# A decoder layer in one kernel: sums of the 64-key softmaxes on GpSimd and logarithms subtracted, the landmark-query softmax transposed, and x1 in place

## The reference

```python
q_l = q.reshape(b, h, m, l, dh).mean(axis=3)          # m = 64 landmarks
k_l = k.reshape(b, h, m, l, dh).mean(axis=3)
attn1 = softmax(q @ k_l.T)                            # 512 tokens x 64 landmark keys
attn2 = softmax(q_l @ k_l.T)                          # 64 x 64
attn3 = softmax(q_l @ k.T)                            # 64 landmark queries x 512 keys
for _ in range(6):                                    # V starts as attn2
    KV = attn2 @ V
    V = 0.25 * V @ (13 * I - KV @ (15 * I - KV @ (7 * I - KV)))
x = x + (attn1 @ (V @ (attn3 @ v))) @ Wout + bout
# cross attention, keys and values from ctx_1024 (64 keys a batch)
scores = where(mask == 0, -1e9, Q @ K.T / sqrt(16))
x = x + (softmax(scores) @ V) @ Wo.T + bo
# feed-forward: sel = argmax(gelu(last @ Wp1 + bp1) @ Wp2 + bp2)
h = gelu(x_norm @ W1[sel] + b1[sel])
x = x + x_norm + 0.3 * ((h @ W2[sel] + b2[sel]) @ Wo_ffn + bo_ffn)
```

## Time and profile before

| | |
|---|---|
| median of three runs | 1453.8 us (1453.03 to 1455.01) |
| the profiled execution | 1456.06 us |
| its span in the trace | 1454.3 us |
| mean granted TensorE clock | 0.992 |
| TensorE busy in the span | 1418.4 us |
| VectorE, ScalarE, GpSimd busy | 1016.4, 752.0, 571.5 us |

### The profile page before, as it was taken

The page is one execution under the profiler, slowest core; times in us unless marked ns, Lnnn a source line. Parts: engine busy times, 40 slices in busy tenths (PEclk is TensorE's granted clock), DMA queues, the critical chain, the costliest instruction groups (busy, mean ns, idle before and its releaser), DMA issues.

```text
span 1454.3 us, 51361 instructions
## 1 busy us (share of the span) xinstructions
PE 1418.4 (98%) x22484; PEld 943.5 (65%) x22484; DVE 1016.4 (70%) x2098; ACT 752.0 (52%) x1460; POOL 571.5 (39%) x784
## 2 busy tenths in 40 slices
PE   8999999999999999999999999999999999999897
PEld 5756666666757667676666767666676666666455
DVE  2567767767677786767778686777867677588651
ACT  2525563655556465555645555564555636544342
POOL 1525361533526144352524435152453613514423
PEclk9999999999999999999999999999999999999899
DMA  8102000101002010100201010010101001100111
GB/s 301 33 3 76 30 31 2 56 12 42 26 4 64 3 42 26 42 25 2 66 2 42 26 42 25 3 61 7 42 26 42 26 2 43 32 3 3 36 48 61
DMA packets 40527, 53.03 MB, mean 36 GB/s; under 512 B 9698, under 2 KB 30450, under 8 KB 40306
## 3 DMA queue, kind: packets, MB, share of 16 engines
q1 hardware_dynamic: 40306, 49.76, 10.6%
HBM read 37.16 MB, written 12.59 MB: 34 GB/s over the span
## 4 chain that ended last, share of the span: by engine, by line
PE 92%; DVE 3%; DMA 1%; ACT 1%; issue 1%; SPq 1%; POOL 1%; DVEq 0%; POOLq 0%; ACTq 0%
PE bank L1207 43%; PE bank L1439 8%; PE bank L1225 7%; PE bank L1235 6%; PE bank L1426 5%; PE bank L1326 3%; PE bank L1394 2%; PE bank L1215 2%; PE bank L1306 2%; PE bank L1335 2%; PE bank L1285 2%; PE bank L1407 2%; PE bank L1385 1%; PE bank L1320 1%; PE bank L1273 1%; PE bank L1428 1%
## 5 line engine op out<-in xcount | busy, mean ns | idle before, releaser
L675 POOL TENSOR_TENSOR b<-ut,eye 128x256 f32<-128x256 f32 x192 | 136.5, 729 | 343.9 <-DVE ut L1047 281.6
L848 ACT ACTIVATE az<-bank 128x320 f32<-128x320 f32 x192 | 67.4, 401 | 159.5 <-PE bank L1225 157.2
L1207 PE MATMUL bank<-xnT_c,w1e 128*128 128x512 f32 x256 | 125.6, 617 | 1.5 <-DMA b1e<-in_b 0.7
L1207 PE MATMUL bank<-xnT_a,wqkv 128*128 128x512 f32 x256 | 125.0, 612 | 0.1
L1103 DVE RECIPROCAL oT_x<-bank 128x256 f32<-128x256 f32 x64 | 107.9, 1725 | 22.9 <-PE bank L1439 22.9
L1207 PE MATMUL bank<-w2e,hT 128*128 128x256 f32 x512 | 119.7, 388 | 0.9 <-ACT hT L908 0.9
L1103 DVE RECIPROCAL oT<-bank 128x256 f32<-128x256 f32 x64 | 111.9, 1751 | 3.5 <-PE bank L1439 2.9
L796 ACT ACTIVATE p<-bank,nm 128x512 f32<-128x512 f32 x128 | 87.3, 691 | 47.0 <-DVE nm L992 46.9
L574 POOL TENSOR_SCALAR var_eps_c<-mv_c 128x2 f32<-128x2 f32 x32 | 7.2, 225 | 255.0 <-DVE mv_c L928 254.9
L1207 PEld LDWEIGHTS bank<-w2e,hT 128*128 128x128 f32 x512 | 95.8, 192 | 16.1 <-issue 1.7
L1077 DVE TENSOR_REDUCE m<-bank 128x8 f32<-128x512 f32 x128 | 79.9, 682 | 27.5 <-PE bank L1394 26.0
(11 more groups left out here) (212 smaller groups left out, 3198.1 us busy)
## 6 DMA issues: line engine op xcount, KB each, us to landing
x_in<-in_x SPq DMA_DIRECT2D x16, 512.0 KB, 4.0
w1e<-in_W SPq DMA_DIRECT2D x16, 512.0 KB, 3.2
w2e<-w2o SPq DMA_DIRECT2D x16, 512.0 KB, 3.8
out<-base SPq DMA_DIRECT2D x32, 256.0 KB, 3.1
row_e<-w2o_row SPq DMA_DIRECT2D x16, 128.0 KB, 4.7
hT<-in_W2T SPq DMA_DIRECT2D x2, 512.0 KB, 5.8
...
```

The lines of the kernel that those rows point to most:

```text
L675: return g.tensor_tensor(b7[:, q, :], ut[:, q, :], eye[28 if it else 7][:].unsqueeze(1) .broadcast_to([P, 4, LM]), ALU.subtract).then_inc( ...
L1207: last = mm(dst, lhsT, rhs, start=(k == 0), stop=(k == len(pairs) - 1))
```

## The change

**The two softmaxes over 64 keys (suffix 1 and x).** The sum is now taken before the transposed maximum. For each of the 8 tiles of a softmax, VectorE's new step `sb` subtracts the maximum from the scores on the way from PSUM to an SBUF tile `ee` (two tiles in turn), ScalarE's `en` exponentiates in place, and GpSimd's `sm` adds 64 values down to 8 in three additions. VectorE's `es` reduces these, ScalarE's `ln` takes the logarithm, and `mp` adds it to the maximum before it splits it in three. What t and e give is then normalised. The steps den, rec and the multiplication of o are gone; ScalarE copies o out of PSUM. The banks of s1 and sx are emptied by `sb`.

**The landmark queries' softmax.** e3 no longer reads the scores s3 and p3T is gone. The maxima m3 (not negated) are split (`mp3`), transposed (`mT3` on TensorE, copied by VectorE) and subtracted in a product, and `t3` computes the scores transposed, as sx does: one starter per tile with `minus3`, then 16 products. e3 exponentiates straight into `p3T`. vt has a column of ones beside each head's 16, which yields the sum, and zT takes the two heads of a pair one after the other.

**x1 in place.** A second transfer loads x into x1 (`S.x1`, after wx of the batch before), `xr` and `x1b` add their biases in place, and the buffers `xr` and `x1_box` are gone. x1b waits for lnB's readers of x1.

**Once, in the first turns.** `cst` makes `minus3`, sets the ones in vt and zeroes `m3_parts`, and v waits for it; a batch whose mask allows no key gets no mask at all (`any_key`).

**The tables.** TURN and LAST are new throughout, and a batch is spread over six turns. One line of each:

```diff
-    S.fc P.k.0-1 D.mx1.1.3-2 S.f.4-3 A.f.3-1 G.b7.1.0-2 P.iT.1-2 P.iZ.1-2 A.mTx-3 P.kx.1-2 D.mx1.1.2-2
+    S.fc D.wb.5.1-6 S.w2.3-5 D.wb.5.0-6 D.sb1.0.3-5 D.vx-6 G.sm1.0.2-5 P.s1.1-5 P.jZ.5-6 A.nmC.0-7
...
```

The core of the rest:

```diff
+                if kind in ("sm1", "smx"):
...
+                    if c := unmet(pool, "A", i, ("en" + x, k, j)):
+                        pool.wait_ge(act_done, c)
+                    if c := unmet(pool, "D", i - 1, ("es" + x,)):
+                        pool.wait_ge(dve_done, c)
+                    e = ee[x][:, j % 2]
+                    for w in (32, 16):
+                        g.tensor_tensor(e[:, :, :, 0:w], e[:, :, :, 0:w], e[:, :, :, w:2 * w], ALU.add)
+                        g.drain()
+                    return g.tensor_tensor(e8[x][:, :, j, 2 * k:2 * k + 2, :], e[:, :, :, 0:8], e[:, :, :, 8:16],
+                                           ALU.add).then_inc(pool_done, 1)
...
-                    return add_row(xr[:], x_in[:], bout_row).then_inc(pool_done, 1)
+                    return add_row(x1[:], x1[:], bout_row).then_inc(pool_done, 1)
...
-                    return s.activation(p3[:, j], tile(i, ("s3", k), j)[:], ACT.Exp, bias=nm3[:, c:c + 1],
-                                        accum_out=sum3[:, c:c + 1]).then_inc(act_done, 1)
...
+                    return s.activation(p3T[:, j].rearrange("p t c -> p (t c)"), tile(i, ("t3", k), j)[:],
+                                        ACT.Exp).then_inc(act_done, 1)
...
+                if kind in ("en1", "enx"):
...
+                    e = ee[x][:, j % 2].rearrange("p t h c -> p (t h c)")
+                    return s.activation(e, e, ACT.Exp).then_inc(act_done, 1)
+                if kind in ("ln1", "lnx"):
...
+                    return s.activation(esum_ln[x][:].rearrange("p t j c -> p (t j c)"),
+                                        esum[x][:].rearrange("p t j c -> p (t j c)"), ACT.Ln).then_inc(act_done, 1)
+                if kind in ("o1", "ox"):
...
+                    return s.activation(oT[x][:, n, :], tile(i, step)[:], ACT.Copy).then_inc(act_done, 1)
...
+                if kind in ("sb1", "sbx"):
...
+                    return v.tensor_tensor(ee[x][:, j % 2], tile(i, ("s" + x, k), j)[:].rearrange(
+                        "p (t h c) -> p t h c", t=T, h=2), m[x][:, :, j, 2 * k:2 * k + 2].unsqueeze(3)
+                        .broadcast_to([P, T, 2, LM]), ALU.subtract).then_inc(dve_done, 1)
+                if kind in ("es1", "esx"):
...
+                    return v.tensor_reduce(esum[x][:].rearrange("p t j c -> p (t j c)"),
+                                           e8[x][:].rearrange("p t j c e -> p (t j c) e"), AX.X, ALU.add).then_inc(dve_done, 1)
...
+                    v.tensor_tensor(m[x][:], m[x][:], esum_ln[x][:], ALU.add)
...
-                    return v.reciprocal(oT[x][:, k, cols], tile(i, ("den" + x, k))[:, cols]).then_inc(dve_done, 1)
...
-                    return v.tensor_tensor(oT[x][:, n, :], tile(i, step)[:], oT[x][:, n, :], ALU.mult).then_inc(dve_done, 1)
...
-                    dst, res = (x1, xr) if kind == "w1" else (x2, x1_box)
+                    dst, res = (x1, x1) if kind == "w1" else (x2, x1)
...
-                        last = nc.tensor.transpose(o[:, t * P:(t + 1) * P], p3[:, n % 4, t * P:(t + 1) * P], ident[:])
+                    for j in range(4):
+                        mm(tile(i, step, j)[:], minus3[rows(j), :], m3T[rows(j), n, :].unsqueeze(1)
+                           .broadcast_to([32, T, P]), start=True, stop=False)
+                    for t in range(T):
+                        for j in range(4):
+                            last = mm(tile(i, step, j)[:, t * P:(t + 1) * P], kT[rows(j), n, t * P:(t + 1) * P],
+                                      flat(qbd[rows(j), n]), start=False, stop=(t == T - 1))
...
-                    for t in range(T):
-                        for j in range(4):
-                            c = (4 * n + j) * 2 * DH
-                            last = mm(o[rows(j), 0:P], vt[:, t, c:c + 2 * DH], p3T[:, j, t, :],
-                                      start=(t == 0), stop=(t == T - 1))
+                    for h in range(2):
+                        q = slice(LM * h, LM * h + LM)
+                        for t in range(T):
+                            for j in range(4):
+                                last = mm(o[rows(j), q], vt[:, t, 2 * (4 * n + j) + h, :], p3T[:, j, t, q],
+                                          start=(t == 0), stop=(t == T - 1))
```

More of the change, by code:

```diff
@@ L172 @@
+    P.wx.1@15 D.wx.1@15 P.wx.0@15 D.lnC.1@15 G.rsC.1@15 D.wx.0@15 A.nmC.1@15 D.lnC.0@15 P.xnTc.1@15
+    A.xnTc.1@15 P.gate@15 A.gate@15 G.rsC.0@15 A.nmC.0@15 P.logit@15 D.logit@15 G.base@15 P.xnTc.0@15
+    A.xnTc.0@15 S.ew1@15 S.ew2@15 G.row@15 P.h.0@15 P.h.1@15 P.h.2@15 A.h.0@15 A.h.1@15 A.h.2@15
+    P.h.3@15 A.h.3@15 P.y3.1@15 D.y3.1@15 P.y3.0@15 D.y3.0@15 S.out.1@15 S.out.0@15
 """
@@ L205, in emptied_by @@
             return step, (0, 1)
[L206 removed]
+        if kind in ("xnTa", "xnTb", "xnTc", "q", "k", "zT", "x2T", "a", "qx", "mT1", "mTx", "o1", "ox", "gate", "h"):
             return step, (0,)
     if engine == "D":
[L209 removed]
+        if kind in ("mx3", "sb1", "sbx"):
             return ("s" + kind[-1], n[0]), (n[1],)
[L211 to L212 removed]
         if kind == "kx":
```

524 lines of the change are left out of this document (287 added, 237 removed).

## The result

The changed kernel takes 1544.3 us (median of four runs, 1543.4 to 1547.0), the kernel before 1454.4 in the same comparison; the ratio is 1.0624 with a 95% interval of 1.0612 to 1.0637. The forecast was 1411.3, within 1384 to 1434. The profiled execution took 1543.38 us, its span is 1541.6. (One slip in the text above: from batch 1 on a batch has 284 steps before and 314 after, not some 330.)

The account below looks back on a forecast made before the run. TensorE, busy 1418.4 of 1454.3 us, was taken as the bound. 1454.3 - 75 + 12 (head) + 5 (steady waits) + 13 (tail) + 2.5 (clock) gave a span of 1411.8, a time of 1411.3 us, range 1384 to 1434.

Parts of the forecast that it names:

- The work that leaves TensorE: TensorE, every batch: sums by ones and p3T transposes go, t3, mT3 and zT halves come; net -4.7 us, -75 over 16.
- its sign of being wrong: TensorE's busy time, expected to fall by about 75 us, falling by less than 60 would point to zT.
- The rival of a dear zT: TensorE's zT: halves cost as much per instruction as whole ones, +1.8 us per batch, 29 in all, about 1440; chance 0.07.
- The head: Start of the program, first pseudo-inverse without projections or den beside it: idle 23.4 us against 11.6, +12.
- The steady waits: Steady turns: small TensorE waits of 0.2 to 0.85 us a turn around iT.3 to jT.3, iZ.5 and s1.1, +5 in all.
- a rival of up to +21: Steady turns: sb, en, sm pass three queues per tile, 0.85 to 1.5 us more a turn, 1423 to 1432; chance 0.15 (to 1437).
- The clock: TensorE's clock: more gaps mean a little more time at 1.2 GHz, +2.5 us.
- The tail: Last batches: new order leaves TensorE waiting 37 us where the kernel before had 24.3 from 150 on, +13.
- the expert's weights: Tail, from logit to h: expert choice and weight load take 6.35 us; waits of 4.6 in batch 14, 5.5 in batch 15.
- The seven table loads: Tail, ScalarE alternating exponential and gelu tables for sx.0 and h of batch 14: 1.28 us each, within a 10 us wait.
- GpSimd's tile: GpSimd's sm, three additions per tile: 1.6 us, with TensorE waiting only from 2.07 us on.
- The rival with GpSimd on the slower side: GpSimd's sm tile is dear: gain used up at 2.45 us a tile, 1470 at 2.6; over 1457 has chance 0.06.

Follow-up runs that it names:

- the first experiment: Changed kernel with waits added on GpSimd in all batches: base waits for mp3 of two batches later, xr for soft2 of the next; 1486.1 us.

## Why the prediction was wrong

**The work that leaves TensorE** (forecast -75): right in kind, some 17 us short: 58 by the steady turns at full clock, 68 at most by the table above. The prediction called 60 its sign of being wrong, and blamed zT for it. But the prices of the named groups hold: the second half of t3 stands 482.31 - 481.09 = 1.22 us ahead of its successor in the first experiment, zT 491.12 - 490.09 = 1.03 (I took 1.1), mT3 0.11. The rival of a dear zT is out. The missing 1.1 us a turn lie in no group that was named. By the distances of starts over the seven turns, o1 and ox, which used to follow a sum of the same form, take 0.4 us more a turn together, and some ten other unchanged groups about 0.1 each. Why they do stays open.

**The head** (forecast +12): right, idle 11.4 to 22.1.

**The steady waits** (forecast +5, with a rival of up to +21): this is the step that failed. From batch 0 to 10 the idle time rose by 53.6 us and the clock's loss by 35.5. The two collisions are most of it: with the waits that keep them apart 58 us came back. I had walked each chain with VectorE's durations from undisturbed rows, and never asked what GpSimd would be doing at that moment. mp3, four small operations, has no price there and no place in a chain at all. The cue was in the trace of before. The scaling of attn2 is 0.69 us in fifteen batches of sixteen and 2.87 once, and its mean of 828 against the 692 of its neighbour is that one:

```profile
1141.54 2.87 DVE L1010 TENSOR_TENSOR attn<-attn,r 128x512 f32<-128x512 f32 x1
...
1141.48 2.38 POOL L597 TENSOR_TENSOR xr<-x_in,bout_row 128x1024 f32<-128x1024 f32 x1
```

(VectorE's and GpSimd's timelines, at the place where LAST takes over from TURN.) The old order kept the two apart in every steady turn; the new one put xr beside attn2 and base and row beside mp3 in most turns (11 of 16 for each pair). Some 6 us of such stalls became some 79, and 11 in the first experiment, summed over VectorE's additions, subtractions, multiplications and casts that read SBUF alone, by what each lasted beyond its own fastest tenth.

The Trainium skill, SBUF — State Buffer, Who interferes with whom, has this rule: a VectorE instruction with two SBUF inputs contends with a GpSimd instruction that reads SBUF. It calls the contention an exclusive lock, for which the order of issue decides who blocks. The traces agree where GpSimd has two inputs, 2.23 us beside 2.35. With one input they agree in part: the subtraction beside the multiplication of 2.78 us was free after 1.07, and L1178 took its 0.22 us at 484.67 beside xn_b, which ran from 484.55 on. I had weighed the engine's speed from the Trainium skill, and not this.

**The clock** (forecast +2.5): mis-sized with the waits. The clock's loss rose by up to 49 us. It follows the waits, as the first experiment shows: with them it left the middle (0.97 to 1.00). A wait of 2.75 us a turn therefore cost about 5 (90.0 - 85.2).

**The tail** (forecast +13, with its clock +15.5): right in its places, too small in size, and the second term that failed. Behind mTx of batch 10 the idle time rose by 42.7 and the clock's loss by 14.5. h to y3 of batch 14 waits 8.34 us, the expert's weights 3.4 (I had 5.5), ox 3.3, the last transposes 3.3. What I missed is one batch earlier: around y3 of batch 13 TensorE waits 1.08, 2.18 and 3.25 us for h's banks and results, and xn_b of batch 15 comes 4.3 and 1.5 us late. The seven table loads, on which most of my 10 us stood, do not set it. The chain that they lie beside does, for the same 10, so that this entry came out right is luck. How the rest of the tail's 57 us divides was not tested.

**GpSimd's tile** (forecast 1.6): 1.76 us from start to start (496.50 to 498.26 in the first experiment): 0.73, 0.46 and 0.32, with 0.1 to 0.15 ahead of each. The rival with GpSimd on the slower side had the right engine with the wrong mechanism. It isn't GpSimd's own lateness that costs here, but what it does to VectorE.

**What the account leaves.** Measured and forecast lie 133 us apart. The collisions are 58 of them, and without them the kernel is still 32 us slower than before and 75 above the forecast. The tail's 42 us beyond its term and the 17 us of work that did not leave are the largest parts of that, read from the traces and not each tested alone.
